# The magic number taken off by TensorE and VectorE instead of Pool in an fp8 rounding stage

## The chip, the cores and the metric
One core of a Trainium2 chip runs the whole kernel. The metric is the device time of one execution in microseconds. The kernel before has a median of 2198.23 us over three runs (2194.11 to 2199.01).

## What is computed
The reference is two transformer layers on x (4 batches x 512 tokens x 512). Only the first of four parts bears on the change:

```python
def _fp8_quant_dequant(x):
    scale = FP8_E4M3_MAX / jnp.maximum(jnp.max(jnp.abs(x)), EPS)
    q = jnp.clip(x * scale, -FP8_E4M3_MAX, FP8_E4M3_MAX).astype(jnp.float8_e4m3fn)
    return q.astype(jnp.float32) / scale
# input = layernorm(x), weight = ctx, bias = mask
out = jnp.einsum('bmk,bkn->bmn', x_dq, w_dq) + bias
x = x + out
```

After it follow a mixture of experts, an attention and a gated feed-forward with a Hadamard transform. They run in later stages of the kernel and are not touched.

## The kernel before
The code writes out, engine by engine, the order of its instructions; there is no planner. Each engine works off its own list and waits on semaphores. The first stage is `batch_product_phase` (L216 to L441); the next stage, `experts_phase`, starts when all engines have left it.

The batches are B = 4 groups of TB = 4 tiles of 128 tokens. SyncE loads x, ctx, the identity and the bias row (broadcast to 128 partitions). VectorE reads the row statistics; the layer norm of three batches is done by ScalarE and of the last by VectorE. VectorE takes the absolute maxima, Pool reduces them over the partitions (L291), and VectorE forms the two scales.

Then eight groups n = 0..7 are quantised, x of batch b being n = 2b and ctx of batch b being n = 2b + 1, each 128 x 2048. The rounding to fp8's three mantissa bits is done by adding and subtracting a large number. ScalarE scales the group (`scale_group`). VectorE's `lift(n)` masks out the exponent of each value (L387), raises it to at least the smallest normal number and multiplies by ROUND_MAGIC (L388), and adds the result to the value (L389). Pool subtracts the same number again and writes bf16 (L303), and VectorE's `clip(n)` bounds the result (L393). TensorE turns the x group with 16 bf16 transposes (L430), ScalarE copies the four turned tiles to SBUF (L337), and TensorE multiplies them with the quantised ctx in 16 matmuls of 512 columns (L438). VectorE's `add(b)` scales the product and adds it to x (L401), and then reads the row statistics of that batch (L102) for the next stage.

Pool adds the bias to x in place (L285): batches 3 and 0 before the all-reduce of the maxima, batch 1 before its first subtraction, batch 2 before its fifth.

In VectorE's list `lift(n)` stands ahead of `clip(n - 1)`, and `add(b - 2)` follows the lift of x of batch b. `scaled`, `magic` and `lifted` have two buffers each, `cq` two, `xq` and `xqT` one.

Two other uses of TensorE with fp32 operands stand in the rows below: `pe.transpose` of fp32 data (L980) and the only plain fp32 `pe.matmul` of the kernel, the router of the experts (L990): 16 tiles times 4 parts, 64 calls, each with 16 moving columns. The products of L52 work on fp32r operands, which a helper splits into a high and a low part.

Of the kernel before, what the change touches and what calls it, by code (L numbers as in the profile page):

```python
# [7 lines left out]
BF16 = mybir.dt.bfloat16  # L8
U32 = mybir.dt.uint32
I32 = mybir.dt.int32  # L10
ALU = mybir.AluOpType
# [3 lines left out]
P = 128  # L15
B, S, D = 4, 512, 512
KD = D // P
# [198 lines left out]
def batch_product_phase(nc, x, ctx_in, bias, consts, x_res, ident, stats):  # L216

    with ExitStack() as ctx:
# [4 lines left out]
        magic = al.sb("magic", [2, TB, D])  # L223
        lifted = al.sb("lifted", [2, TB, D])
        neg_mean = al.sb("neg_mean", [NT])
        xq = al.sb("xq", [TB, D], BF16)
        cq = al.sb("cq", [2, TB, D], BF16)
        xqT = al.sb("xqT", [KD, S], BF16)
        bias_bc = al.sb("bias_bc", [B, D])
        ident_bf = al.sb("ident_bf", [P], BF16)  # L230
# [16 lines left out]
        centred = al.sem("centred")  # L247
        xn_ready = al.sem("xn_ready")
        xn_last = al.sem("xn_last")
        biased = al.sem("biased")  # L250
# [5 lines left out]
        lowered = al.sem("lowered")  # L256
        quant_ready = al.sem("quant_ready")
# [6 lines left out]
        BIAS_ORDER = [B - 1, *range(B - 1)]  # L264
        quantised = lambda n: cq[:, n // 2 % 2] if n % 2 else xq[:, :, :]

        @block.sync
        def _(sp):
# [8 lines left out]
        @block.gpsimd  # L277
        def _(pool):
            pool.wait_ge(bias_in, 16 * B)

            def add_bias(b):
# [6 lines left out]
            for b in BIAS_ORDER[:2]:  # L288
                add_bias(b)
            pool.wait_ge(amax_ready, 1)  # L290
            nc.gpsimd.partition_all_reduce(amax_all[:, :], amax[:, :], P,  # L291
                                           bass.bass_isa.ReduceOp.max).then_inc(amax_over, 1)

            for n in range(2 * B):
                b = n // 2
                if n in (0, 4):
                    add_bias(BIAS_ORDER[2 if n == 0 else 3])
                pool.wait_ge(lifted_ready, n + 1)
                if n % 2 == 0 and b > 0:
                    pool.wait_ge(turned, TB * b)  # L300
                if n % 2 == 1 and b > 1:
                    pool.wait_ge(product, TB * (b - 1))
                pool.tensor_tensor(quantised(n), lifted[:, n % 2], magic[:, n % 2], ALU.subtract).then_inc(lowered, 1)  # L303

        @block.scalar
        def _(act):
            act.wait_ge(neg_mean_ready, 1)
            for g in range(B - 1):
                batch = range(TB * g, TB * g + TB)
                for i in batch:  # L310
                    ins = act.activation(xn[:, i, :], x_res[:, i, :], ACT.Identity, bias=neg_mean[:, i:i + 1])
                ins.then_inc(centred, 1)
                act.wait_ge(centred, g + 1)
# [12 lines left out]

            scale_group(0, xn[:, 0:TB, :], 0)
            scale_group(1, raw[:, 0:TB, :], 1)
            for b in range(B):
                if b + 1 < B:  # L330
                    scale_group(2 * b + 2, xn[:, TB * b + TB:TB * b + 2 * TB, :], 0)
                    scale_group(2 * b + 3, raw[:, TB * b + TB:TB * b + 2 * TB, :], 1)
                if b > 0:
                    act.wait_ge(product, TB * b)
                for t in range(TB):
                    act.wait_ge(turned, TB * b + t + 1)
                    act.activation(xqT[:, :, t * P:(t + 1) * P], turn[t].rearrange("p (k t) -> p k t", k=KD),  # L337
                                   ACT.Copy).then_inc(turned_out, 1)

        @block.vector  # L340
        def _(dve):
# [7 lines left out]
            def batch_amax(which, values, g):  # L349
                return dve.tensor_reduce(amax_parts[:, which, g:g + 1], values[:, TB * g:TB * g + TB, :], AX.XY,  # L350
                                         ALU.max, apply_absolute_value=True)

            for g in range(B):
                dve.wait_ge(x_in[g], 16)
# [21 lines left out]
            dve.wait_ge(scale_ready, 1)  # L376
            link(dve.tensor_tensor(unscale[:, 0:1], scale[:, 0:1], scale[:, 1:2], ALU.mult))
            link(dve.reciprocal(unscale[:, 1:2], unscale[:, 0:1]))

            def lift(n):
                y, m = scaled[:, n % 2], magic[:, n % 2]
# [7 lines left out]
            def clip(n):  # L391
                dve.wait_ge(lowered, n + 1)
                dve.tensor_scalar(quantised(n), quantised(n), FP8_MAX, -FP8_MAX, ALU.min,  # L393
                                  ALU.max).then_inc(quant_ready, 1)

            def add(b):
                dve.wait_ge(biased, BIAS_ORDER.index(b) + 1)
# [6 lines left out]
            lift(0)  # L404
            for n in range(1, 2 * B):
                lift(n)
                clip(n - 1)
                if n >= 4 and n % 2 == 0:
                    add(n // 2 - 2)
                    dve.wait_ge(added, TB * (n // 2 - 1))  # L410
                    stats.read(dve, n // 2 - 2)
            add(B - 2)
            dve.wait_ge(added, TB * (B - 1))
            stats.read(dve, B - 2)
            clip(2 * B - 1)
            stats.finish(dve, 0, B - 1)
            add(B - 1)
            dve.wait_ge(added, NT)
# [3 lines left out]
        def _(pe):  # L422
            pe.wait_ge(const_ready, 1)
            for b in range(B):
                pe.wait_ge(quant_ready, 2 * b + 1)
# [6 lines left out]
                pe.wait_ge(turned_out, TB * (b + 1))  # L432
                pe.wait_ge(quant_ready, 2 * b + 2)
                for t in range(TB):
                    if b > 0:
                        pe.wait_ge(added, TB * (b - 1) + t + 1)
                    for k in range(KD):
                        ins = pe.matmul(banks[t][:, :], xqT[:, k, t * P:(t + 1) * P], cq[:, b % 2, k, :],  # L438
                                        start=(k == 0), stop=(k == KD - 1))
                    ins.then_inc(product, 1)  # L440
    return al.sems  # L441
# [1553 lines left out]
```

## Time and profile before

| | us |
|---|---|
| median of three runs | 2198.23 |
| the profiled execution's own time | 2198.48 |
| its span | 2196.9 |
| TensorE busy | 1963.6 (89%) |
| VectorE busy | 1346.1 (61%) |
| ScalarE busy | 826.8 (38%) |
| Pool busy | 1042.5 (47%) |

The span is the time from the first to the last instruction in the profile; the execution's own time is what the runs' times are compared with. Busy times of a whole kernel are a mean over stages: the first stage takes about the first 145 us, and in it TensorE is mostly idle.

### The profile page before, as it was taken

The page shows a single profiled execution, that of the slowest core. Times are in us where ns is not written, and L with a number is a line of the kernel's source. Part 1 is how long each engine was busy: PE and PEld are TensorE (multiplying, and loading weights), DVE is VectorE, ACT ScalarE, POOL GpSimd, SP SyncE. Part 2 cuts the span into 40 slices and gives each one's busy share as a digit, 9 for nine tenths or more (in the row PEclk, how much of TensorE's full clock was granted, in tenths as well). Part 3 has the DMA queues.
Part 4 walks back from the last instruction along what each step waited for, and adds up shares of the span by engine and source line. Part 5 has one row for each costly group of instructions (what it writes and reads, how often), then busy time and mean ns, then how long its engine had stood idle before and what let it go on. Part 6 is the DMA issues. An engine that isn't in the chain of part 4 may idle for free. (4 is left out here: it accounts for less than half of the span.)

```text
span 2196.9 us, 28789 instructions
## 1 busy us (share of the span) xinstructions
PE 1963.6 (89%) x9721; PEld 1633.4 (74%) x9721; DVE 1346.1 (61%) x2080; ACT 826.8 (38%) x1610; POOL 1042.5 (47%) x837
## 2 busy tenths in 40 slices
PE   0259988784999999999999999999979999999999
PEld 0147766673788888888888888888857788888887
DVE  7885488887677666666776666666666333333333
ACT  4233277772444444444544444444432111111111
POOL 2733635633676666566765666666543222102200
PEclk9869999997999999999999999999999999999999
DMA  4037499984566555556555555555541000000002
GB/s 173 0 118 290 166 320 366 363 312 144 177 184 177 158 148 160 165 148 175 157 162 164 148 160 167 152 149 166 140 121 48 29 29 29 10 19 29 0 1 77
DMA packets 163357, 313.11 MB, mean 143 GB/s; under 512 B 15680, under 2 KB 41024, under 8 KB 163264
## 3 DMA queue, kind: packets, MB, share of 16 engines
q1 hardware_dynamic: 145856, 253.18, 37.6%
q0 software_dynamic: 17408, 58.73, 8.2%
q8 instruction: 53, 0.87, 0.2%
q14 instruction: 40, 0.33, 0.0%
HBM read 203.33 MB, written 108.53 MB: 142 GB/s over the span
## 5 line engine op out<-in xcount | busy, mean ns | idle before, releaser
L1289 POOL TENSOR_TENSOR t_pT_lo<-t_pT_raw,t_pT_hi 128x512 fp32r<-128x512 f32 x256 | 327.3, 1300 | 245.2 <-ACT t_pT_hi L1380 243.4
L1475 DVE TENSOR_REDUCE t_sums<-t_score 128x1 f32<-128x512 f32 x256 | 169.8, 688 | 146.6 <-PE t_score L52 146.5
L1835 DVE TENSOR_TENSOR f_lin<-f_lin,f_silu 128x512 f32<-128x512 f32 x64 | 44.7, 699 | 287.0 <-PE f_lin L52 287.0
L1393 ACT ACTIVATE t_probs<-t_score,t_sums 128x512 f32<-128x512 f32 x256 | 175.0, 683 | 82.7 <-DVE t_sums L1475 67.5
L1465 DVE STREAM_TRANSPOSE t_blocks<-t_probs 128x512 f32<-128x512 f32 x256 | 172.7, 694 | 23.4 <-ACT t_probs L1393 23.1
L1760 POOL TENSOR_TENSOR f_w_hi<-w_raw,f_zeros 128x1024 fp32r<-128x1024 f32 x16 | 30.4, 1903 | 318.3 <-PE f_gate L52 314.8
L1457 DVE SCALAR_TENSOR_TENSOR x_res<-t_out,t_sums,x_res 128x512 f32<-128x512 f32 x256 | 179.2, 741 | 3.7 <-PE t_out L52 3.7
L1380 ACT ACTIVATE t_pT_hi<-t_pT_raw 128x512 fp32r<-128x512 f32 x256 | 160.3, 626 | 5.1 <-DMA t_pT_raw<-turned_blocks 5.1
L1793 ACT ACTIVATE f_silu<-f_gate 128x512 f32<-128x512 f32 x64 | 38.3, 598 | 303.9 <-PE f_gate L52 303.9
L52 PE MATMUL t_score<-t_wv_hi,t_cT_hi 128*128 128x256 f32 x512 | 144.9, 283 | 2.0 <-ACT t_probs L1393 2.0
L52 PE MATMUL t_score<-t_wv_hi,t_cT_lo 128*128 128x256 f32 x512 | 145.0, 283 | 0.0
L52 PE MATMUL t_score<-t_wv_lo,t_cT_hi 128*128 128x256 f32 x512 | 145.0, 283 | 0.0
L1374 ACT ACTIVATE t_o_hi<-t_o 128x512 fp32r<-128x512 f32 x64 | 38.3, 598 | 224.7 <-PE t_o L52 224.7
L1440 DVE TENSOR_TENSOR t_k_lo<-t_score,t_k_hi 128x512 fp32r<-128x512 f32 x64 | 44.3, 692 | 123.5 <-ACT t_k_hi L1365 123.5
L1365 ACT ACTIVATE t_k_hi<-t_score 128x512 fp32r<-128x512 f32 x64 | 38.3, 598 | 212.7 <-PE t_score L52 212.7
L1855 DVE TENSOR_TENSOR x_res<-f_down,x_res 128x512 f32<-128x512 f32 x128 | 87.9, 689 | 42.9 <-PE f_down L52 42.9
L52 PE MATMUL t_score<-t_cT_hi,t_wk_hi 128*128 128x512 f32 x256 | 101.3, 396 | 11.4 <-DVE t_cT_lo L1536 11.4
L52 PE MATMUL t_out<-t_wo_hi,t_o_hi 128*128 128x512 f32 x256 | 103.3, 403 | 8.0 <-DVE t_o_lo L1450 6.3
L52 PE MATMUL t_score<-t_k_hi,t_q_hi 128*128 128x512 f32 x256 | 102.2, 399 | 7.8 <-DVE t_q_lo L1435 4.1
L52 PE MATMUL f_gate<-f_xT_hi,f_w_hi 128*128 128x512 f32 x256 | 101.2, 395 | 8.6 <-POOL f_w_lo L1763 5.5
L52 PE MATMUL t_o<-t_pT_hi,t_v_hi 128*128 128x512 f32 x256 | 100.1, 391 | 4.0 <-POOL t_pT_lo L1289 4.0
L52 PE MATMUL t_q<-t_xT_hi,t_wq_hi 128*128 128x512 f32 x256 | 101.0, 394 | 2.8 <-DVE t_xT_lo L212 2.8
(280 smaller groups left out, 6057.0 us busy)
## 6 DMA issues: line engine op xcount, KB each, us to landing
turned_blocks<-t_blocks SPq DMA_DIRECT2D x256, 256.0 KB, 3.6
t_pT_raw<-turned_blocks SPq DMA_DIRECT2D x256, 256.0 KB, 4.2
e_up_raw<-in_L_ffn_Wrt_up_dram SPq DMA_DIRECT2D x47, 512.0 KB, 7.1
e_down_raw<-in_L_ffn_Wrt_down_dram SPq DMA_DIRECT2D x47, 512.0 KB, 6.3
tokens_by_expert<-e_xg SPq DMA_DIRECT2D x1, 12032.0 KB, 41.1
e_xg<-tokens_by_expert SPq DMA_DIRECT2D x47, 256.0 KB, 6.7
outputs_by_expert<-e_y_out SPq DMA_DIRECT2D x47, 256.0 KB, 7.0
wq_raw<-in_L_xattn_Wq_dram POOLq DMA_DIRECT2D x32, 256.0 KB, 4.3
```

The source lines that it names most:

```text
L52: ins = pe.matmul(out, w(k), x(k), start=(k == 0 and j == 0), stop=(k == k_tiles - 1 and j == 2))
L1289: pool.tensor_tensor(pT_lo[:, q], pT_raw[:, q], f32(pT_hi[:, q]), ALU.subtract).then_inc(p_ready, 1)
L1365: act.activation(k_hi[:, :], score_bank[0][:, :], ACT.Copy).then_inc(k_hi_ready, 1)
L1374: act.activation(o_hi[:, :].rearrange("p (u q j) -> p q u j", q=Q4, j=BLK), o_bank[:, :].rearrange("p (q u j) -> p q u j", q=Q4, j=BLK), A ...
L1380: act.activation(pT_hi[:, q], pT_raw[:, q], ACT.Copy).then_inc(p_hi_ready, 1)
L1393: act.activation(probs[:, t % 2, :], score_bank[t][:, :], ACT.Exp, bias=neg_max[:, t:t + 1], accum_out=inv[:, p, t:t + 1]).then_inc(exp_re ...
L1440: dve.tensor_tensor(k_lo[:, :], score_bank[0][:, :], f32(k_hi[:, :]), ALU.subtract).then_inc(k_ready, 1)
L1457: dve.scalar_tensor_tensor(out=x_tile, in0=out_bank[t % 2][:, :], scalar=inv[:, p, t:t + 1], in1=x_tile, op0=ALU.mult, op1=ALU.add).then_i ...
L1465: dve.transpose(blocks[:, :, :, t, :].rearrange("p a t j -> p t a j"), probs[:, t % 2, :].rearrange("p (t a j) -> p t a j", a=Q4, j=BLK)). ...
L1475: dve.tensor_reduce(neg_max[:, t:t + 1], score_bank[t][:, :], AX.X, ALU.max, negate=True).then_inc(max_ready, 1)
L1835: dve.tensor_tensor(lin_bank[k][:, :], lin_bank[k][:, :], silu[:, k, :], ALU.mult).then_inc(mid_done, 1)
L1855: dve.tensor_tensor(x_tile, down_bank[t][:, :], x_tile, ALU.add).then_inc(added, 1)
```

## The change
Pool's subtraction is gone. `lift` keeps three instructions, but the multiplication by ROUND_MAGIC moves from the second to the third, so that the buffer (now `power`) holds the bare power of two. For x, TensorE turns the lifted value with the identity and adds to the same PSUM tile the turned power times an identity scaled by -ROUND_MAGIC, both as plain fp32 matmuls; the four turn banks are fp32. ScalarE copies them to bf16 as before, and VectorE clips the turned x in one instruction (`clip_x`). For ctx, VectorE takes the magic off itself (`lower_c`) and clips. Two of the four bias additions move from Pool to VectorE. `xqT` has two buffers. VectorE's order per batch is now lift x, lift ctx, lower ctx, clip x, add of the batch before, statistics.

```diff
-        xqT = al.sb("xqT", [KD, S], BF16)
+        xqT = al.sb("xqT", [2, KD, S], BF16)
...
-        turn = [al.ps(f"turn{t}", [KD * P], BF16) for t in range(TB)]
+        turn = [al.ps(f"turn{t}", [KD * P]) for t in range(TB)]
...
+        POOL_BIAS, VECTOR_BIAS = (B - 1, 0), (1, 2)
...
-            for n in range(2 * B):
-                b = n // 2
-                if n in (0, 4):
-                    add_bias(BIAS_ORDER[2 if n == 0 else 3])
-                pool.wait_ge(lifted_ready, n + 1)
-                if n % 2 == 0 and b > 0:
-                    pool.wait_ge(turned, TB * b)
-                if n % 2 == 1 and b > 1:
-                    pool.wait_ge(product, TB * (b - 1))
-                pool.tensor_tensor(quantised(n), lifted[:, n % 2], magic[:, n % 2], ALU.subtract).then_inc(lowered, 1)
...
-            act.activation(ident_bf[:, :], ident[:, :], ACT.Copy).then_inc(const_ready, 1)
+            act.activation(lower_ident[:, :], ident[:, :], ACT.Copy, scale=-ROUND_MAGIC).then_inc(const_ready, 1)
...
             dve.tensor_reduce(amax[:, :], amax_parts[:, :, :], AX.X, ALU.max).then_inc(amax_ready, 1)
+            add_bias(VECTOR_BIAS[0])
             dve.wait_ge(amax_over, 1)
...
             link(dve.reciprocal(unscale[:, 1:2], unscale[:, 0:1]))
+            add_bias(VECTOR_BIAS[1])
+            dve.wait_ge(biased_here, 2)
...
                 dve.wait_ge(scaled_ready, n + 1)
-                if n >= 2:
-                    dve.wait_ge(lowered, n - 1)
+                if n >= 2 and n % 2 == 0:
+                    dve.wait_ge(turned, TB * (n // 2))
                 link(dve.tensor_scalar(m.bitcast(U32), y.bitcast(U32), EXPONENT_BITS, None, ALU.bitwise_and))
-                link(dve.tensor_scalar(m, m, FP8_MIN_NORMAL, ROUND_MAGIC, ALU.max, ALU.mult))
-                dve.tensor_tensor(lifted[:, n % 2], y, m, ALU.add).then_inc(lifted_ready, 1)
...
+                link(dve.tensor_scalar(m, m, FP8_MIN_NORMAL, None, ALU.max))
+                dve.scalar_tensor_tensor(out=lifted[:, n % 2], in0=m, scalar=ROUND_MAGIC, in1=y, op0=ALU.mult,
+                                         op1=ALU.add).then_inc(lifted_ready, 1)
+
+            def lower_c(b):
+                q = cq[:, b % 2]
+                dve.wait_ge(lifted_ready, 2 * b + 2)
+                if b > 1:
+                    dve.wait_ge(product, TB * (b - 1))
+                link(dve.scalar_tensor_tensor(out=q, in0=power[:, 1], scalar=-ROUND_MAGIC, in1=lifted[:, 1], op0=ALU.mult,
+                                              op1=ALU.add))
+                dve.tensor_scalar(q, q, FP8_MAX, -FP8_MAX, ALU.min, ALU.max).then_inc(c_ready, 1)
+
+            def clip_x(b):
+                q = xqT[:, b % 2]
+                dve.wait_ge(turned_out, TB * (b + 1))
+                dve.tensor_scalar(q, q, FP8_MAX, -FP8_MAX, ALU.min, ALU.max).then_inc(x_ready, 1)
...
+            for b in range(B):
+                lift(2 * b)
+                lift(2 * b + 1)
+                lower_c(b)
+                clip_x(b)
+                if b > 0:
+                    add(b - 1)
+                    dve.wait_ge(added, TB * b)
+                    stats.read(dve, b - 1)
...
-                        ins = pe.transpose(turn[t][:, k * P:(k + 1) * P], xq[:, t, k * P:(k + 1) * P], ident_bf[:, :])
+                        ks = slice(k * P, (k + 1) * P)
+                        pe.matmul(turn[t][:, ks], lifted[:, 0, t, ks], ident[:, :], start=True, stop=False)
+                        ins = pe.matmul(turn[t][:, ks], power[:, 0, t, ks], lower_ident[:, :], start=False, stop=True)
```

## Rows read from the trace of the kernel before

**Rows 1.** Windows: stretch, us; busy (x) of PE, PEld, DVE, ACT, POOL; clock; DMA.
```profile
47.50:144.80 97.30, 28.38 (x128) 13.02 (x128) 90.06 (x91) 21.89 (x23) 56.70 (x16) 0.78 0.00 0
```

**Rows 2.** Timeline at the stage's end: start, duration, engine, line, operation, [idle before].
```profile
145.31 4.54 DVE L880 TENSOR_SCALAR e_xn<-x_res,mean_var,rstd 128x512 f32<-128x512 f32 x8 [0.55 <-PEq L218]
```

**Rows 3.** Groups by form, VectorE, 0 to 165 us: busy us, mean ns, idle before.
```profile
L387 DVE TENSOR_SCALAR a_magic<-a_scaled 128x2048 uint32<-128x2048 uint32 x8 | 24.1, 3014 | 1.8 <-ACT a_scaled L324 1.7
L389 DVE TENSOR_TENSOR a_lifted<-a_scaled,a_magic 128x2048 f32<-128x2048 f32 x8 | 20.2, 2527 | 0.3
L388 DVE TENSOR_SCALAR a_magic<-a_magic 128x2048 f32<-128x2048 f32 x8 | 11.7, 1462 | 0.3
L393 DVE TENSOR_SCALAR a_xq<-a_xq 128x2048 bf16<-128x2048 bf16 x4 | 7.0, 1758 | 5.6 <-POOL a_xq L303 5.6
L393 DVE TENSOR_SCALAR a_cq<-a_cq 128x2048 bf16<-128x2048 bf16 x4 | 3.8, 954 | 0.0
```

**Rows 4.** The timeline of VectorE and Pool from 70.5 us.
```profile
70.56 1.22 DVE L387 TENSOR_SCALAR a_magic<-a_scaled 128x2048 uint32<-128x2048 uint32 x1
...
71.81 1.23 DVE L388 TENSOR_SCALAR a_magic<-a_magic 128x2048 f32<-128x2048 f32 x1
73.08 2.29 DVE L389 TENSOR_TENSOR a_lifted<-a_scaled,a_magic 128x2048 f32<-128x2048 f32 x1
75.28 0.69 DVE L393 TENSOR_SCALAR a_cq<-a_cq 128x2048 bf16<-128x2048 bf16 x1
...
75.45 4.90 POOL L303 TENSOR_TENSOR a_xq<-a_lifted,a_magic 128x2048 bf16<-128x2048 f32 x1 [5.36 <-DVE a_lifted L389]
75.89 5.55 DVE L387 TENSOR_SCALAR a_magic<-a_scaled 128x2048 uint32<-128x2048 uint32 x1
...
98.15 2.72 DVE L401 SCALAR_TENSOR_TENSOR x_res<-a_out,a_unscale,x_res 128x512 f32<-128x512 f32 x4
```

**Rows 5.** The timeline around the scales, and one page row for a 128x512 addition's size.
```profile
44.85 0.17 DVE L373 TENSOR_SCALAR a_amax<-a_amax_all 128x2 f32<-128x2 f32 x1 [3.23 <-POOL a_amax_all L291]
47.56 1.23 DVE L387 TENSOR_SCALAR a_magic<-a_scaled 128x2048 uint32<-128x2048 uint32 x1 [1.75 <-ACT a_scaled L324]
...
L1835 DVE TENSOR_TENSOR f_lin<-f_lin,f_silu 128x512 f32<-128x512 f32 x64 | 44.7, 699 | 287.0 <-PE f_lin L52 287.0
```

**Rows 6.** The timeline of ScalarE in the batch of 85 us.
```profile
85.06 2.00 ACT L324 ACTIVATE a_scaled<-a_ctx_raw,a_scale 128x2048 f32<-128x2048 f32 x1 [7.65 <-DVE a_lifted L389]
86.97 2.04 ACT L337 ACTIVATE a_xqT<-a_turn 128x512 bf16<-128x512 bf16 x4
```

**Rows 7.** Groups by form, whole kernel and 145 to 160 us: fp32 matmuls, weight loads.
```profile
L990 PE MATMUL e_bank<-e_router_raw,e_x 128*128 128x16 f32 x128 | 17.9, 289 | 0.0
L980 PE MATMUL e_bank<-ident,e_xn 128*128 128x128 f32 x64 | 11.3, 354 | 4.4 <-DVE e_xn L880 4.4
...
L990 PEld LDWEIGHTS e_bank<-e_router_raw,e_x 128*128 128x128 f32 x60 | 6.9, 192 | 0.0
```

**Rows 8.** The timeline of fp32 bursts; tile queries (starts); windows with granted clock.
```profile
151.79 3.64 PE L990 MATMUL e_bank<-e_router_raw,e_x 128*128 128x16 f32 x32
155.29 1.94 PE L980 MATMUL e_bank<-ident,e_xn 128*128 128x128 f32 x16
...
L990 PE MATMUL e_bank<-e_router_raw,e_x x20: 263/374/376, 167.6 to 171.5; 128*128 128x16 f32 x20
...
L980 PE MATMUL e_bank<-ident,e_xn x22: 401/421/472, 145.9 to 150.5; 128*128 128x128 f32 x22
...
167.80:171.70 3.90, 3.90 (x20) 0.50 1.05 410
```

**Rows 9.** The timeline of split products and of this stage's last turn.
```profile
704.46 0.28 PE L52 MATMUL t_score<-t_wv_hi,t_cT_hi 128*128 128x256 f32 x1
...
705.17 0.28 PE L52 MATMUL t_score<-t_wv_hi,t_cT_hi 128*128 128x256 f32 x1
...
129.41 1.17 PE L430 MATMUL a_turn<-a_ident_bf,a_xq 128*128 128x128 bf16 x16 [4.35 <-DVE a_xq L393]
```

More of the change, by code:

```diff
@@ L222, in batch_product_phase @@
         scaled = al.sb("scaled", [2, TB, D])
[L223 removed]
+        power = al.sb("power", [2, TB, D])
         lifted = al.sb("lifted", [2, TB, D])
         neg_mean = al.sb("neg_mean", [NT])
[L226 removed]
         cq = al.sb("cq", [2, TB, D], BF16)
[L228 removed]
+        xqT = al.sb("xqT", [2, KD, S], BF16)
         bias_bc = al.sb("bias_bc", [B, D])
[L230 removed]
+        lower_ident = al.sb("lower_ident", [P])
         amax_parts = al.sb("amax_parts", [2, B])
@@ L249, in batch_product_phase @@
         xn_last = al.sem("xn_last")
-        biased = al.sem("biased")
+        biased, biased_here = al.sem("biased"), al.sem("biased_here")
         amax_ready = al.sem("amax_ready")
@@ L255, in batch_product_phase @@
         lifted_ready = al.sem("lifted_ready")
-        lowered = al.sem("lowered")
-        quant_ready = al.sem("quant_ready")
+        c_ready = al.sem("c_ready")
+        x_ready = al.sem("x_ready")
         turned = al.sem("turned")
@@ L263, in batch_product_phase @@
         tiles = lambda a, g: a[g].rearrange("(t p) d -> p t d", p=P)
-        BIAS_ORDER = [B - 1, *range(B - 1)]
-        quantised = lambda n: cq[:, n // 2 % 2] if n % 2 else xq[:, :, :]
+        POOL_BIAS, VECTOR_BIAS = (B - 1, 0), (1, 2)
         @block.sync
@@ L279, in _ @@
             pool.wait_ge(bias_in, 16 * B)
-            def add_bias(b):
+            for b in POOL_BIAS:
                 pool.wait_ge(*((xn_ready, b + 1) if b + 1 < B else (xn_last, 1)))
@@ L286, in add_bias @@
                 ins.then_inc(biased, 1)
-            for b in BIAS_ORDER[:2]:
-                add_bias(b)
             pool.wait_ge(amax_ready, 1)
@@ L332, in _ @@
                     scale_group(2 * b + 3, raw[:, TB * b + TB:TB * b + 2 * TB, :], 1)
-                if b > 0:
-                    act.wait_ge(product, TB * b)
+                if b > 1:
+                    act.wait_ge(product, TB * (b - 1))
                 for t in range(TB):
                     act.wait_ge(turned, TB * b + t + 1)
-                    act.activation(xqT[:, :, t * P:(t + 1) * P], turn[t].rearrange("p (k t) -> p k t", k=KD),
+                    act.activation(xqT[:, b % 2, :, t * P:(t + 1) * P], turn[t].rearrange("p (k t) -> p k t", k=KD),
                                    ACT.Copy).then_inc(turned_out, 1)
@@ L351, in batch_amax, with add_bias @@
                                          ALU.max, apply_absolute_value=True)
+            def add_bias(b):
+                dve.wait_ge(bias_in, 16 * B)
+                for t in range(TB):
+                    x_tile = x_res[:, TB * b + t, :]
+                    ins = dve.tensor_tensor(x_tile, x_tile, bias_bc[:, b, :], ALU.add)
+                ins.then_inc(biased_here, 1)
             for g in range(B):
@@ L378, in _ @@
             link(dve.reciprocal(unscale[:, 1:2], unscale[:, 0:1]))
+            add_bias(VECTOR_BIAS[1])
+            dve.wait_ge(biased_here, 2)
             def lift(n):
-                y, m = scaled[:, n % 2], magic[:, n % 2]
+                y, m = scaled[:, n % 2], power[:, n % 2]
                 dve.wait_ge(scaled_ready, n + 1)
-                if n >= 2:
-                    dve.wait_ge(lowered, n - 1)
+                if n >= 2 and n % 2 == 0:
+                    dve.wait_ge(turned, TB * (n // 2))
                 link(dve.tensor_scalar(m.bitcast(U32), y.bitcast(U32), EXPONENT_BITS, None, ALU.bitwise_and))
-                link(dve.tensor_scalar(m, m, FP8_MIN_NORMAL, ROUND_MAGIC, ALU.max, ALU.mult))
-                dve.tensor_tensor(lifted[:, n % 2], y, m, ALU.add).then_inc(lifted_ready, 1)
[L391 to L394, printed above, removed]
+                link(dve.tensor_scalar(m, m, FP8_MIN_NORMAL, None, ALU.max))
[4 more added lines that the diff above has]
+                dve.wait_ge(lifted_ready, 2 * b + 2)
+                if b > 1:
+                    dve.wait_ge(product, TB * (b - 1))
[6 more added lines that the diff above has]
+                dve.tensor_scalar(q, q, FP8_MAX, -FP8_MAX, ALU.min, ALU.max).then_inc(x_ready, 1)
             def add(b):
-                dve.wait_ge(biased, BIAS_ORDER.index(b) + 1)
+                dve.wait_ge(biased, len(POOL_BIAS))
                 for t in range(TB):
@@ L402, in add @@
                                              in1=x_res[:, i, :], op0=ALU.mult, op1=ALU.add).then_inc(added, 1)
[L404 to L415, printed above, removed]
+            for b in range(B):
[7 more added lines that the diff above has]
+                    stats.read(dve, b - 1)
             stats.finish(dve, 0, B - 1)
@@ L424, in _ @@
             for b in range(B):
-                pe.wait_ge(quant_ready, 2 * b + 1)
+                pe.wait_ge(lifted_ready, 2 * b + 1)
                 for t in range(TB):
@@ L429, in _ @@
                     for k in range(KD):
-                        ins = pe.transpose(turn[t][:, k * P:(k + 1) * P], xq[:, t, k * P:(k + 1) * P], ident_bf[:, :])
+                        ks = slice(k * P, (k + 1) * P)
+                        pe.matmul(turn[t][:, ks], lifted[:, 0, t, ks], ident[:, :], start=True, stop=False)
+                        ins = pe.matmul(turn[t][:, ks], power[:, 0, t, ks], lower_ident[:, :], start=False, stop=True)
                     ins.then_inc(turned, 1)
-                pe.wait_ge(turned_out, TB * (b + 1))
-                pe.wait_ge(quant_ready, 2 * b + 2)
+                pe.wait_ge(c_ready, b + 1)
+                pe.wait_ge(x_ready, b + 1)
                 for t in range(TB):
@@ L437, in _ @@
                     for k in range(KD):
-                        ins = pe.matmul(banks[t][:, :], xqT[:, k, t * P:(t + 1) * P], cq[:, b % 2, k, :],
+                        ins = pe.matmul(banks[t][:, :], xqT[:, b % 2, k, t * P:(t + 1) * P], cq[:, b % 2, k, :],
                                         start=(k == 0), stop=(k == KD - 1))
```

## The prediction

> **What bounds the kernel now.** I read the page's busy shares first, then the windows of the first stage, the groups of instructions by form in that stage, its timeline, and last TensorE's rows for fp32 operands wherever the kernel has them. The change lies wholly in the first stage, and the chain that ended last names no line of it, so what binds here has to be read from the stage itself. From the first rounding instruction to the last row statistics VectorE works 90.06 of 97.30 us while TensorE has 28.38 and ScalarE 21.89 [rows 1]. VectorE's last statistics end at 144.76 (145.31 less 0.55 of idle), and what releases its first instruction of stage two is the branch at the barrier [rows 2]. What the first stage ends earlier or later should therefore move the whole rest, one for one.
>
> VectorE's 90 us are not all its own work. The same masking instruction L387 takes 1.22 us at 70.56, when Pool is idle, and 5.55 us at 75.89, when a Pool subtraction of 4.90 us has just begun; it ends 1.1 us after Pool does, as if it had waited for Pool's end [rows 4]. So I take a clean time for each form from [rows 4] and compare it with the group sums of [rows 3].
>
> **Term A, what goes.** The groups L387, L388, L389 and the two of L393 take 24.1 + 11.7 + 20.2 + 7.0 + 3.8 = 66.8 us [rows 3]. Without Pool beside them: 8 x (1.22 + 1.23 + 2.29) + 8 x 0.69 = 43.4 [rows 4]. Both lifts stay three instructions of the same size, and both clips stay (the x clip moves behind the turn, same 128x2048 bf16 shape), so the gain is 23.4. VectorE's wait for Pool's subtraction goes too, 5.6 [rows 3]. A = -29.0. The subtraction on Pool itself (eight like the 4.90 at 75.45) is gone with nobody waiting for it.
>
> **Term B, what VectorE gets.** lower_c is a fused multiply-add of 128x2048 fp32 into bf16, four times. The fused form appears at 128x512 as 2.72 for four, PSUM operand included, and the plain fp32 tensor_tensor at 128x2048 takes 2.29 [rows 4]. Bounds 2.29 and 2.72; I take 2.29, the same element count without PSUM. With its link: 4 x 2.33 = +9.3. The last multiplication of the lift moves from the second instruction into the third; both sizes and counts of passes are as before, so 0.
>
> **Term C, the bias.** Two of Pool's four bias batches go to VectorE, 4 x 0.70 = 2.8 us each, by the 128x512 fp32 tensor_tensor [rows 5]. The first stands where VectorE idles 3.23 before the all-reduce's answer at 44.85 [rows 5]: hidden. If Pool's all-reduce is slowed by it, at most doubled, that is +3. The second stands where VectorE now waits 1.75 for ScalarE's scaled x [rows 5]: 2.8 - 1.75 = +1.05, and the wait for its own writes makes it +1.1. No DMA moves: SyncE's queue issues what it did, and the bias rows have landed well before 44.85, since Pool, which waits for them first of all, answers then.
>
> **Term D, the new wait.** clip_x(b) sits in VectorE's queue and waits for turned_out, that is for TensorE's turn in fp32 and ScalarE's copies. Behind it are queued add, the row statistics, the next lift, and TensorE's product. Count from L, the end of lift(2b). VectorE reaches clip_x at L + 4.72 (lift(2b+1), 70.56 to 75.28) + 2.33 + 0.65 = L + 7.7. ScalarE scales the next context group from L + 4.8 to L + 6.8 and then needs 2.04 for four copies [rows 6]: L + 8.9 at best, a floor of 1.2 us of waiting in the first three batches.
>
> TensorE is the unknown. The code issues 32 plain fp32 matmuls a batch. L990 is the only plain fp32 matmul in the trace: 64 in the code, 128 records, so each is two records with a weight load each, where the 64 fp32 transposes of L980 are 64 records [rows 7]. So 64 records a batch. Their pitch: L990, with only 16 moving columns, (3.64 - 0.26) / 31 = 0.109 us in a warm stretch, and about 0.21 at the half clock (20 records from 167.6 to 171.5, granted 0.50, 1.2 of 2.4 GHz) [rows 8]. That hardly depends on the columns, since the transposes with 128 columns have the same two pitches, (1.94 - 0.27) / 15 = 0.111, and 22 records from 145.9 to 150.5, 0.22: the weight load sets L990's pitch. A load's record there lasts 192 ns, reaching over the next load's start [rows 7]. In the split products of 256 columns, one load each, the pitch is (705.17 - 704.46) / 6 = 0.118 [rows 9]: there 256 columns stream under one load. If a record of the new turn streams its 128 columns twice, it is that same case: 0.118. Bounds: below 0.109, above load and stream not overlapped, 0.109 + 0.109 = 0.218.
>
> The clock: between product and turn TensorE will rest some 4 to 6 us. After a rest of 4.4 before 145.91 L980 starts at a pitch of 0.22 and keeps it 4.6 us [rows 7, 8]. I take 4.5 us, 21 records, at 1.2 GHz and 43 at 2.4: 4.5 + 43 x 0.118 + 0.27 = 9.85. The copy of the last tile is out at L + 0.1 + 9.85 + 0.6 + 0.1 = L + 10.65, so clip_x waits 2.95. Four batches: D = +11.8. Product and add keep their places and hide as before: product(3) runs beside add(2), the statistics and the finish, 9 us for its 6.
>
> The Trainium skill has a rule that speaks against the change: "TensorE: Matmul & The Clock Gate", section "Terms", says transpose mode makes fp32 four times faster, and the change gives that mode up. Taken at its word a plain one would cost 4 x 0.109 = 0.436, two records of 0.218, rival 2 below. "FP8 and Floating Point Precision", section "TensorE Precision Notes", counts four passes for true fp32, two a record, which would fit under the load and give the sum above. No row here decides between them.
>
> **Sum.** -29.0 + 9.3 + 1.1 + 11.8 = -6.8. The profiled execution took 2198.48 around a span of 2196.9, 0.25 above the median of the three runs, 2198.23. 2198.48 - 6.8 = 2191.7.
>
> **Rivals.**
> 1. The turn is cheaper: TensorE stays at 2.4 GHz and the pitch is 0.109. 64 x 0.109 + 0.27 = 7.25, the copies end at ScalarE's floor, waits 1.2 x 3 and 0.35 in the last: 3.95 for 11.8, so 2183.8. For it: the turn at 129.41 ran 16 bf16 records in 1.17, warm after a rest of 4.3 [rows 9]. Against: the rest before 145.91.
> 2. The slower side: load and stream don't overlap, 0.218 a record, 0.43 at the low clock. 4.5 + 53.5 x 0.218 + 0.27 = 16.4, wait 9.5 a batch, 38.0 for 11.8: +19.4, 2218. VectorE then waits on TensorE. It decides from where the waits sum over 18.6, 4.65 a batch, a turn of 11.55 us. For it: no row shows 128 plain columns. Against: L990's pitch equals one load, so loads do run under streams.
> 3. Pitch as forecast, but the clock never rises in the turn: 64 x 0.213 = 13.6 + 0.27, wait 7.0, sum 28: +9.4, 2208. Against: L980 rises within its burst.
> 4. No change: the clock rises 8 us into the turn, or the pitch is some 0.145: wait 4.5, sum 18, 2198. Also where Pool isn't what stretches L387, half of A gone and the turn short.
>
> **How the numbers follow.** Forecast 0.59, its own range 2188 to 2195 (clock 3 to 6.5 us low, waits 2.3 to 3.8, 2 us of scatter); rival 1 0.10; rival 2 0.11; rival 3 0.07; rival 4 0.13. 0.2% is 4.4 us, what can be told from no change here. Faster: nearly all of the first two cases less the forecast's edge, 0.66. Within: rival 4 and that edge, 0.16. Slower: rivals 2 and 3, 0.18. The range 2183.5 to 2204 leaves out rival 2, most of rival 3 and the low end of rival 1.
>
> **What would show it.** In the stage's groups after: L387's counterpart at 1.22 mean and no instruction over 3 us; lower_c at 2.3; 256 records of the turn at 0.12 pitch once the clock is granted; VectorE idle before clip_x about 3 us four times, released by ScalarE's copy; second stage starting near 138.5. A turn of over 11.5 us a batch, or masks still over 2 us with Pool silent, would make it wrong.

## The result, and the profile after

The kernel after takes 2184.02 us, the median of four runs (2180.46 to 2187.84); the kernel before, four runs on the same chip, 2197.65 (2194.11 to 2199.01). The ratio is 0.9941 with a 95% interval of 0.992 to 0.9961: about 13 us faster, more than the 4.4 us that this kernel's measurement can tell from nothing. The forecast was 2191.7. The profiled executions took 2180.46 after and 2198.48 before. Of all executions behind the ratios below one is left out as disturbed, of bias_only: 3075.57 us, where its eleven others took 2218 to 2230.

The windows of the first stage after, from its first mask to its last statistics, answer to [rows 1]; columns as there.

```profile
48.39:132.68 84.29, 47.58 (x316) 39.23 (x320) 76.23 (x95) 21.43 (x23) 0.00 (x0) 0.91 0.00 0
```

VectorE's busy time falls from 90.06 to 76.23, Pool's from 56.70 to nothing, and TensorE's rises from 28.38 to 47.58. VectorE is still the engine that sets the length, but in 8 us of the 84 it now stands idle.

The groups by form on VectorE from 44 to 165 us after, answering to [rows 3]: busy us, mean ns, then idle before.

```profile
L382 DVE SCALAR_TENSOR_TENSOR a_lifted<-a_power,a_scaled 128x2048 f32<-128x2048 f32 x8 | 18.3, 2293 | 0.3
L381 DVE TENSOR_SCALAR a_power<-a_power 128x2048 f32<-128x2048 f32 x8 | 9.8, 1227 | 0.3
L380 DVE TENSOR_SCALAR a_power<-a_scaled 128x2048 uint32<-128x2048 uint32 x8 | 9.8, 1222 | 0.1
L390 DVE SCALAR_TENSOR_TENSOR a_cq<-a_power,a_lifted 128x2048 bf16<-128x2048 f32 x4 | 9.2, 2292 | 0.1
L397 DVE TENSOR_SCALAR a_xqT<-a_xqT 128x2048 bf16<-128x2048 bf16 x4 | 2.8, 694 | 6.5 <-ACT a_xqT L321 6.5
L392 DVE TENSOR_SCALAR a_cq<-a_cq 128x2048 bf16<-128x2048 bf16 x4 | 2.8, 694 | 0.1
```

The mask has gone from a mean of 3014 ns to 1222, and every form now has one duration. The one new idle time is the 6.5 us ahead of the clip of the turned x, L397, released by ScalarE's copy.

The timeline after, at the places of [rows 5], [rows 6] and [rows 2] and at the four waits.

```profile
44.86 0.17 DVE L365 TENSOR_SCALAR a_amax<-a_amax_all 128x2 f32<-128x2 f32 x1 [1.14 <-POOL a_amax_all L286]
45.85 2.50 DVE L341 TENSOR_TENSOR x_res<-x_res,a_bias_bc 128x512 f32<-128x512 f32 x4
48.39 1.23 DVE L380 TENSOR_SCALAR a_power<-a_scaled 128x2048 uint32<-128x2048 uint32 x1
62.92 0.69 DVE L397 TENSOR_SCALAR a_xqT<-a_xqT 128x2048 bf16<-128x2048 bf16 x1 [1.94 <-ACT a_xqT L321]
75.01 2.04 ACT L321 ACTIVATE a_xqT<-a_turn 128x512 bf16<-128x512 f32 x4
77.08 0.69 DVE L397 TENSOR_SCALAR a_xqT<-a_xqT 128x2048 bf16<-128x2048 bf16 x1 [0.96 <-ACT a_xqT L321]
97.24 0.69 DVE L397 TENSOR_SCALAR a_xqT<-a_xqT 128x2048 bf16<-128x2048 bf16 x1 [1.70 <-ACT a_xqT L321]
117.56 0.69 DVE L397 TENSOR_SCALAR a_xqT<-a_xqT 128x2048 bf16<-128x2048 bf16 x1 [1.85 <-ACT a_xqT L321]
133.23 4.54 DVE L882 TENSOR_SCALAR e_xn<-x_res,mean_var,rstd 128x512 f32<-128x512 f32 x8 [0.55 <-PEq L218]
```

The stage ends at 133.23 - 0.55 = 132.68, 12.1 us earlier than the 144.76 of before. The profiled spans differ by 18.1 (2196.9 and 2178.8). The other 6 lie in later stages: from the experts to the attention 239.2 us before and 236.2 after, from there to the feed-forward 1145.4 and 1142.3. Over all kernels profiled here these two stretches range over 236.2 to 241.1 and 1141.6 to 1145.4, with nothing in them changed. Two more profiles of the changed kernel (after_again and after_third below) have 239.7 and 1144.9, 238.6 and 1145.3, so the shorter stretches of this one are scatter. What the change did by the profiles is the 12.1; the 13.6 between the medians agrees with it within the interval.

The windows of PE in the four turns after: stretch and length, busy (records), granted clock, DMA share, GB/s. (A turn is TensorE's 64 records for one batch.) The first row is nearly the whole of the second turn, the other two pairs are the third and the fourth, each cut where its clock rose.

```profile
68.70:75.50 6.80, 6.80 (x63) 1.00 0.01 2
...
87.85:90.50 2.65, 2.65 (x12) 0.50 0.00 0
90.60:96.30 5.70, 5.70 (x53) 0.99 0.01 3
...
108.00:111.10 3.10, 3.10 (x14) 0.50 0.00 0
111.20:116.60 5.40, 5.40 (x50) 1.00 0.00 0
```

All of it is 64 records a batch, about 0.11 us apart at 2.4 GHz and 0.21 to 0.22 at 1.2. The four turns last 8.91, 7.42, 8.77 and 8.90 us, with some 3.1, 0.3, 2.7 and 3.15 of them at the lower pace. For the third and fourth the granted clock of the rows says so. For the first two it doesn't, the view has 1.00 throughout: the first turn's 3.1 us are read from its records, which start 0.213 apart until 56.5 and 0.112 after, and in the second only the first record is followed after 0.21, which costs 0.1 us.

### The profile page after: what moved, and what is told of

It reads as the page before. It is cut to its first block and busy times, and to the rows that moved or that the text cites. A ratio compares the mean times of both kernels' runs of the same rounds, so it can differ in the third digit from the quotient of the medians.

```text
span 2178.8 us, 29158 instructions
## 1 busy us (share of the span) xinstructions
PE 1979.0 (91%) x9909; PEld 1655.4 (76%) x9913; DVE 1338.5 (61%) x2092; ACT 826.4 (38%) x1610; POOL 991.1 (45%) x821
```

## The experiments

A kernel's ratio is to the kernel before on the same chip, with its 95% interval. Times of different chips are not compared: where half_turn, double_turn, warm and pool_beside ran, the kernel before takes 2198, elsewhere some 2226, with the expert stage about 28 us longer in every kernel. Stage one is compared by the start of stage two, the first `e_xn` row of the timeline, which is 133.23 in the change.

**The change again, twice.**

> The changed kernel once more, beside the other three on one chip. The first stage ended at 144.76 us before and at 132.68 after, 12.1 earlier; the profiled spans differ by 18.1. Theory (all of the gain is made in the first stage): the ratio to before is 1 - 12.1/2198 = 0.9945, 2186 us, and the 6 us more of the profiled pair are scatter of the expert stage. Rival (something behind the first stage gains too): ratio near 0.992, 2180 us.

> The changed kernel once more, as the measure for the two beside it: stage one over at 132.7 to 134.3, the second stage's wait for the router 28.94 us after its start, ratio to before 0.993 to 0.9945.

after_again: 0.9926 (0.9903 to 0.9949), stage two starts at 134.80, waits 2.72, 0.96, 1.98 and 2.13. after_third: 0.9954 (0.9936 to 0.9972), 133.17, waits 1.91, 0.96, 1.68 and 1.85. Both intervals hold the 0.9945 of the stage alone; that of after_again holds the rival's 0.992 too, that of after_third doesn't. Between copies of one kernel the start of stage two moves by 1.6 us, 1.4 of it through the three waits that hang on the turn (the first turn of after_again took 9.69 us); the 0.96 stays.

**Is it Pool's silence? Pool kept busy with work that nobody waits for.**

```diff
+            for n in range(2 * B):
+                pool.wait_ge(lifted_ready, n + 1)
+                pool.wait_ge(idle_done, n) if n else None
+                pool.tensor_tensor(idle_out[:, :, :], bias_bc[:, :, :], bias_bc[:, :, :], ALU.subtract).then_inc(idle_done, 1)
```

> The changed kernel, and beside it Pool does a 128x2048 fp32 subtraction into an unused bf16 tile each time a lift is done, as it did before the change; nobody waits for it. Theory (Pool's mere running stretches VectorE): the mask after each lift of x goes from 1.2 to 5.5 and the ctx clip is held to Pool's end, some 4.3 + 2.6 a batch, 27.6 us, less the waits that it covers, 6.45: stage end near 154, ratio to before 1.004. Rival (the stretch came from what both touched, or the gain came from shorter dependencies): VectorE's instructions stay at 1.22 and 2.29, ratio 0.9945.

1.0062 (1.0048 to 1.0077), slower than before; stage two starts at 152.54, 19.3 us later than in the profile of after. The profiled execution took 2201.83, the other three 2210.39 to 2213.16; what the further 9 to 11 us are, no profile shows. The timeline of VectorE and Pool in it:

```profile
97.61 1.22 DVE L386 TENSOR_SCALAR a_power<-a_scaled 128x2048 uint32<-128x2048 uint32 x1
97.77 4.51 POOL L293 TENSOR_TENSOR a_idle_out<-a_bias_bc 128x2048 bf16<-128x2048 f32 x1 [11.22 <-DVE a_lifted L388]
98.86 4.50 DVE L387 TENSOR_SCALAR a_power<-a_power 128x2048 f32<-128x2048 f32 x1
...
105.73 2.29 DVE L396 SCALAR_TENSOR_TENSOR a_cq<-a_power,a_lifted 128x2048 bf16<-128x2048 f32 x1
105.77 5.70 POOL L293 TENSOR_TENSOR a_idle_out<-a_bias_bc 128x2048 bf16<-128x2048 f32 x1 [3.49 <-DVE a_lifted L388]
108.05 3.97 DVE L398 TENSOR_SCALAR a_cq<-a_cq 128x2048 bf16<-128x2048 bf16 x1
```

The mask that began before Pool's instruction keeps its 1.22. The tensor_scalar that begins after it takes 4.50 for 1.23 and ends at 103.36, 1.08 after Pool's 102.28: it waits for Pool's end. The fused instruction with two inputs runs beside Pool in its usual 2.29, and there it is Pool that pays, 5.70 for 4.51. The clip that follows it, L398, begins during Pool's instruction and is held again, 3.97 for 0.69. The buffers are unrelated, so no dependence of data does this. The Trainium skill says this under "SBUF — State Buffer", section "Who interferes with whom": GpSimd and a tensor_scalar of VectorE in its faster mode exclude each other for a whole instruction, and whichever has begun first keeps the port. The trace agrees, with 4.50 for 1.23.

**One part alone: the bias of batches 1 and 2 to VectorE in the kernel before.**

```diff
...
             dve.tensor_reduce(amax[:, :], amax_parts[:, :, :], AX.X, ALU.max).then_inc(amax_ready, 1)
+            add_bias(VECTOR_BIAS[0])
...
+            add_bias(VECTOR_BIAS[1])
+            dve.wait_ge(biased_here, 2)
```

In Pool's list, which stands earlier in the file:

```diff
-                if n in (0, 4):
-                    add_bias(BIAS_ORDER[2 if n == 0 else 3])
```

> The kernel before with one part of the change alone: the bias of batches 1 and 2 is added by VectorE at the same places as in the changed kernel; Pool still subtracts the magic. Theory: VectorE's wait of 5.6 us for Pool's first subtraction goes, and the stretches beside Pool's two long bias additions; the masks beside Pool's subtractions stay at 5.5. Counted through, the stage ends near 138.2, 6.6 earlier, ratio 0.997. Rival (Pool's subtraction is the whole cost): no gain beyond 1 us, ratio 1.0.

0.9963 (0.9946 to 0.9981); stage two starts at 138.57, 6.7 us before [rows 2]. So about half of the gain needs neither TensorE's part nor Pool's leaving the subtraction, only two bias additions moved. VectorE no longer waits for Pool's subtraction, because Pool is never behind, but it is stretched nearly as before: its rounding groups sum to 64.9 us where [rows 3] have 66.8. The group of its mask in bias_only, and one meeting with Pool in its timeline:

```profile
L395 DVE TENSOR_SCALAR a_magic<-a_scaled 128x2048 uint32<-128x2048 uint32 x8 | 27.1, 3384 | 0.1
```

```profile
53.70 5.40 POOL L301 TENSOR_TENSOR a_xq<-a_lifted,a_magic 128x2048 bf16<-128x2048 f32 x1 [8.47 <-DVE a_lifted L397]
54.78 5.41 DVE L396 TENSOR_SCALAR a_magic<-a_magic 128x2048 f32<-128x2048 f32 x1
```

Here L396 ends 1.09 after Pool does, once more.

**The other way to free Pool: VectorE lowers x as it lowers the context, and TensorE turns bf16.**

```diff
+            def lower_x(b):
+                q = xq[:, :, :]
...
+                link(dve.scalar_tensor_tensor(out=q, in0=power[:, 0], scalar=-ROUND_MAGIC, in1=lifted[:, 0], op0=ALU.mult,
+                                              op1=ALU.add))
                 dve.tensor_scalar(q, q, FP8_MAX, -FP8_MAX, ALU.min, ALU.max).then_inc(x_ready, 1)
...
-                        pe.matmul(turn[t][:, ks], lifted[:, 0, t, ks], ident[:, :], start=True, stop=False)
-                        ins = pe.matmul(turn[t][:, ks], power[:, 0, t, ks], lower_ident[:, :], start=False, stop=True)
+                        ins = pe.transpose(turn[t][:, k * P:(k + 1) * P], xq[:, t, k * P:(k + 1) * P], ident_bf[:, :])
```

> The changed kernel with TensorE's part undone: VectorE takes the magic off x as well (a fourth fused instruction per batch, 2.29 us, and a clip of bf16 before the turn), TensorE turns bf16 as before; Pool stays out. Theory (the gain comes from Pool's leaving, TensorE's subtraction only saves 4 x 2.33 us of VectorE less the 6.45 us of waits): stage end 48.4 + 61.6 + 15.8 + 9.3 = 135.0, +2.3 against the changed kernel, ratio to before 0.9955. Rival (TensorE's part carries the gain): the stage ends near 144 again, ratio 1.0.

0.9962 (0.9944 to 0.9981); stage two starts at 136.19, 1.4 us after after_again and 3.0 after after_third. The group of the added instruction:

```profile
L398 DVE SCALAR_TENSOR_TENSOR a_xq<-a_power,a_lifted 128x2048 bf16<-128x2048 f32 x4 | 9.2, 2292 | 0.1
```

That is 9.2 us of VectorE's own work in place of 6.45 to 7.8 of waits for the turn: TensorE's share in the change is worth 1.4 to 3 us. The rest, 9.1 us from [rows 2], comes with Pool out of the loop, whether the magic is then taken off by TensorE or by VectorE; bias_only has 6.7 of them with Pool still subtracting. The intervals of the ratios overlap with those of the change, so it is read from the starts alone.

**What does the turn cost VectorE? The turn halved and doubled.** half_turn leaves out the second matmul of each pair (so the large number stays on x), double_turn issues each pair twice.

```diff
-                        pe.matmul(turn[t][:, ks], lifted[:, 0, t, ks], ident[:, :], start=True, stop=False)
-                        ins = pe.matmul(turn[t][:, ks], power[:, 0, t, ks], lower_ident[:, :], start=False, stop=True)
+                        ins = pe.matmul(turn[t][:, ks], lifted[:, 0, t, ks], ident[:, :], start=True, stop=True)
```

> The changed kernel without the second matmul of each pair (the magic stays on x: that part of the computation is left out). The turn halves to 64 records less 32: about 5.4 us cold, 3.8 warm. Theory (VectorE's wait at the clip is the longer of TensorE's turn and ScalarE's copies, and ScalarE alone leaves a floor of about 1 us in batches 0 to 2): waits 1.2 + 1 + 1 + 0 for 6.45, stage end near 129.4, 3.3 earlier, ratio to before 0.993. Rival (there is no floor, TensorE alone sets the wait): waits 0, 126.2.

> The changed kernel with every pair of turning matmuls issued twice (same result), 128 records a batch. Theory (above 6.95 us every us of the turn is a us of waiting): turn 3.3 + 112 x 0.1115 + 0.3 = 16.1 cold-started and 14.5 warm, waits 9.1 or 7.5, 33 to 37 us in sum for 6.45, stage end near 161, 28 later, ratio to before about 1.007. Rival (the wait is soaked up elsewhere, by the add and the statistics behind it): under 15 us later.

half_turn: 0.9923 (0.9909 to 0.9938), start of stage two 129.74. double_turn: 1.0083 (1.0063 to 1.0103), 162.77. The clips' rows, first of half_turn, then of double_turn:

```profile
62.11 0.69 DVE L397 TENSOR_SCALAR a_xqT<-a_xqT 128x2048 bf16<-128x2048 bf16 x1 [0.96 <-ACT a_xqT L321]
...
114.07 0.69 DVE L397 TENSOR_SCALAR a_xqT<-a_xqT 128x2048 bf16<-128x2048 bf16 x1
```

```profile
71.01 0.69 DVE L397 TENSOR_SCALAR a_xqT<-a_xqT 128x2048 bf16<-128x2048 bf16 x1 [10.05 <-ACT a_xqT L321]
91.70 0.69 DVE L397 TENSOR_SCALAR a_xqT<-a_xqT 128x2048 bf16<-128x2048 bf16 x1 [7.50 <-ACT a_xqT L321]
```

With the turn out of the way 0.96 is left three times and nothing the fourth: that is ScalarE, which scales the next context before it copies, and has none to scale in the last batch. Stage two starts 3.5 us earlier than in after, for 6.45 - 2.88 = 3.6 less of waiting. (In this profile stage two then loses more than that again, see late_clip below.) Twice the turn brings 29.5 us, for 36.00 - 6.45 = 29.55 more of waiting. So the waits go into the length of the stage one for one, and the turn counts only above ScalarE's floor.

**What does a record cost, by its columns?** Plain fp32 matmuls of eight widths, twelve of each, ahead of the first turn, behind twenty of 128 columns.

```diff
...
+            for n in (16, 64, 96, 128):
+                for f in range(12):
+                    pe.matmul(turn[f % TB][:, 0:n], ident[:, :], ident[:, 0:n], start=True, stop=True)
+            for n in (192, 256, 384, 512):
+                for f in range(12):
+                    pe.matmul(turn[f % TB][:, 0:n], ident[:, :], bias_bc[:, 0, 0:n], start=True, stop=True)
```

> The changed kernel with bursts of 12 plain fp32 matmuls (24 records) of 16, 64, 96, 128, 192, 256, 384 and 512 moving columns on TensorE ahead of the first turn, behind 20 of 128 columns that raise the clock; only the pitch of records within a burst is read, the kernel's own time means nothing. Theory (a record is the longer of a weight load of 0.107 us and two streams of its columns at 2.4 GHz): 0.11 up to 128 columns, 0.160 at 192, 0.213 at 256, 0.320 at 384, 0.427 at 512. Rival (load and stream add up, at one column a cycle in sum 0.107 for 128): pitch falls below 0.09 at 64 and 16 columns and grows evenly, 0.16 at 256, 0.27 at 512. Rival (four streams a record): 0.213 already at 128.

Only its rows are read. TensorE's records by tile in narrow stretches: line, count, shortest/median/longest in ns, first and last start, forms.

```profile
L429 PE MATMUL a_turn<-ident x26: 274/276/352, 54.6 to 57.5; 128*128 128x128 f32 x24, 128*128 128x96 f32 x2
L432 PE MATMUL a_turn<-a_bias_bc,ident x24: 326/327/328, 57.7 to 61.4; 128*128 128x192 f32 x24
L432 PE MATMUL a_turn<-a_bias_bc,ident x24: 326/380/380, 61.4 to 66.3; 128*128 128x256 f32 x23, 128*128 128x192 f32 x1
L432 PE MATMUL a_turn<-a_bias_bc,ident x25: 379/487/487, 66.5 to 74.2; 128*128 128x384 f32 x24, 128*128 128x256 f32 x1
L432 PE MATMUL a_turn<-a_bias_bc,ident x25: 486/593/593, 74.2 to 84.3; 128*128 128x512 f32 x24, 128*128 128x384 f32 x1
```

Each matmul is two records. Their pitch at 2.4 GHz is 0.112 us at 128 columns, 0.1625 at 192, 0.216 at 256, 0.3225 at 384 and 0.429 at 512. From 192 on that is two cycles of 2.4 GHz a column: 2 x 192 / 2400 = 0.160, 2 x 512 / 2400 = 0.427. At 128 columns it would be 0.107, but the bursts of 16 and 64 columns stood at 0.112 as well, and the router's 16 at 0.109 [rows 8]. So a record takes two cycles a column and never less than about 0.11. That this floor is the load of the next weights, which lies beside the stream, fits these numbers; no run varies the load alone. "FP8 and Floating Point Precision" of the Trainium skill, section "TensorE Precision Notes", counts four passes for true fp32; two records of two cycles a column are four, and this trace agrees. The Trainium skill's rule in "TensorE: Matmul & The Clock Gate", section "Terms", that transpose mode is four times faster in fp32, does not hold at 128 columns: two records of 0.1115 are 0.223, twice the 0.111 of a transpose [rows 8].

The windows of PE in columns. The first runs from the middle of the burst of 64 columns to near the end of that of 96, the second over that of 128; before 47.9 the bursts of 16 and 64 columns ran at a granted 1.00.

```profile
48.00:54.60 6.60, 6.60 (x33) 0.50 0.00 0
55.00:57.60 2.60, 2.60 (x26) 1.00 0.00 0
```

**Can the clock be held up? Filler matmuls ahead of each turn.**

```diff
+                if b > 0:
+                    pe.wait_ge(turned_out, TB * b)
+                for f in range(50 if b == 0 else 16):
+                    pe.matmul(turn[f % TB][:, 0:P], ident[:, :], ident[:, :], start=True, stop=True)
```

> The changed kernel with filler matmuls on TensorE (50 plain fp32 ones before the first turn, 16 before each other, into the same banks, overwritten). Theory (the turns of batches 0, 2 and 3 lose 1.3 to 1.6 us each to the low clock): turns all 7.4 us, waits at ScalarE's floor 1.1 x 3 + 0.5, 3.6 for 6.45, stage end near 130, ratio to before 0.993. Rival (fillers delay the turns, or the clock doesn't rise for them): no gain or a loss against 0.9945.

0.9957 (0.9938 to 0.9975); stage two starts at 132.53, waits 1.98, 2.64, 0.96 and 0.35, in sum 5.93 for 6.45, and no gain in time over the change. The theory mostly failed. In the first batch the fillers ended at 50.57, TensorE rested 2.50, and then the clock fell inside the turn, from 54.5 to 57.7; before the second turn, which needs no help, the fillers delayed it. The last two turns did fall to their floors.

**Can the wait be filled? The clip moved behind the add and the statistics of the batch before.**

```diff
-                clip_x(b)
                 if b > 0:
                     add(b - 1)
                     dve.wait_ge(added, TB * b)
                     stats.read(dve, b - 1)
+                clip_x(b)
```

> VectorE's clip of the turned x stands behind the add and the statistics of the batch before, instead of ahead of them; nothing else. Theory (VectorE's waits at the clip, 0.96 + 1.70 + 1.85 us in batches 1 to 3, are the only cost of the turn, and 5.2 us of other work covers them): the stage ends 4.5 earlier, at 128.2, ratio to before 0.9925; batch 0 keeps its wait of 1.9. TensorE's rest before each turn shrinks from 5.6 to about 1, so the turn starts at 2.4 GHz. Rival (the later clip makes the product late for the add, or delays the next turn): the wait moves to the add, no gain over the changed kernel, 0.9945.

0.9936 (0.991 to 0.9961), against 0.9926 of after_again beside it: no gain. Yet the stage is shorter, with waits of 3.01, 0, 0 and 0. TensorE goes into the last two turns almost without a rest, and they take 7.31 us each, with no record at the low pace. Rows of late_clip:

```profile
129.93 4.50 DVE L882 TENSOR_SCALAR e_xn<-x_res,mean_var,rstd 128x512 f32<-128x512 f32 x8 [0.90 <-PEq L218]
...
130.78 5.29 PE L982 MATMUL e_bank<-ident,e_xn 128*128 128x128 f32 x32 [5.38 <-DVE e_xn L882]
148.59 13.67 PE L992 MATMUL e_bank<-e_router_raw,e_x 128*128 128x16 f32 x64
...
162.30 0.43 DVE L831 TENSOR_REDUCE e_top<-e_bank 128x16 f32<-128x256 f32 x1 [17.49 <-PE e_bank L992]
```

The same in after:

```profile
133.84 5.96 PE L982 MATMUL e_bank<-ident,e_xn 128*128 128x128 f32 x32 [11.16 <-DVE e_xn L882]
...
151.57 10.56 PE L992 MATMUL e_bank<-e_router_raw,e_x 128*128 128x16 f32 x64
...
162.17 0.42 DVE L831 TENSOR_REDUCE e_top<-e_bank 128x16 f32<-128x256 f32 x1 [14.01 <-PE e_bank L992]
```

Stage two starts 4.9 us before after_again's, and `e_top`, which needs the router, comes 32.37 us after that start, not 28.94: the last 64 router records take 13.67 for 10.56, the pitch of the lower clock. In after, before and six of the other profiles it is 28.94 or 28.95, in warm 28.91. But half_turn has 35.24 (its profiled execution took 2187.5, two of its others 2179), and columns has 38.35, though it starts stage two last of all, at 164.41. So an early end of stage one alone doesn't explain the loss.

**Late only in batches 1 and 2, so that TensorE's rest before stage two is as in the change; and the same with a bias addition in batch 0's wait.**

```diff
+                late = b in (1, 2)
+                if not late:
+                    clip_x(b)
...
+                if late:
+                    clip_x(b)
```

> The late clip only in batches 1 and 2; batches 0 and 3 as in the changed kernel. Theory (the late clip of all three batches won 4.9 us in stage one and lost 3.4 again at the router of stage two, because TensorE then rested only 5.4 us ahead of that stage and its clock fell at another place): with batch 3's clip early TensorE's rest before stage two is 11 us again, the router's wait 28.94, and stage one still ends 2.7 to 2.9 earlier: ratio 0.0013 under the changed kernel's. Rival (any earlier end of stage one is given back at the router): router's wait 31 to 32, ratio equal to the changed kernel's.

> As late_mid, and VectorE's bias of batch 2 stands in its wait for the first turn (1.9 to 3.0 us) instead of ahead of the first lift. Theory: the first lift starts at 47.6 instead of 48.4, the wait of batch 0 takes the 2.5 us of the bias: 0.4 to 0.8 us less than late_mid. Rival (the turn starts 0.8 earlier only, and the wait outlasts the bias): within 0.3 of late_mid.

late_mid: 0.9951 (0.9932 to 0.997), late_mid_bias: 0.995 (0.993 to 0.997), beside after_third's 0.9954. Stage two starts at 131.02 and 130.20, waits 2.78, 0, 0, 1.37 and 0.70, 0, 0, 1.47. The bias in the wait brought the 0.8 expected of it. In late_mid the rest was restored, 11.15 us, and the clock was not. The timeline and window of late_mid:

```profile
131.62 6.37 PE L986 MATMUL e_bank<-ident,e_xn 128*128 128x128 f32 x32 [11.15 <-DVE e_xn L886]
155.65 13.67 PE L996 MATMUL e_bank<-e_router_raw,e_x 128*128 128x16 f32 x64
...
169.36 0.42 DVE L835 TENSOR_REDUCE e_top<-e_bank 128x16 f32<-128x256 f32 x1 [23.41 <-PE e_bank L996]
```

```profile
144.00:169.00 25.00, 25.00 (x121) 0.50 1.05 411
```

From 144 on TensorE runs at a granted 0.50, 96 of the router's 128 records in it, and `e_top` comes 38.34 us after the stage's start (38.35 in late_mid_bias). My theory, that the length of TensorE's rest before stage two decides this, fell; after one and the same rest of 9.48 us warm has 28.91, half_turn 35.24 and columns 38.35. The runs of late_mid go from 2207.0 to 2220.8, those of after_third from 2210.1 to 2225.3. Six runs of late_mid took 2217.4 or more and one 2207.0, about the 9.4 us that the profiled one lost at the router; whether that one kept its clock, no profile shows. So none of the three orders is seen to beat the change in time, though they start stage two 2.1 to 3.2 us earlier than its best copy. What sets the router's clock stays open.

## Why the prediction was right, and where it was off

Direction and path were forecast well, the size only to a factor of two: 13.6 us by the medians where 6.5 were forecast, 12.1 in the stage where 6.8 were. The 2184.02 lies inside the stated range by 0.5 us at its lower end, one of the four runs lies below it, and the forecast's own case, 2188 to 2195 with a chance of 0.59, did not come. That the time fell inside is in part luck.

What binds and where it ends: right. Stage one ends earlier and stage two follows it, 28.94 us to `e_top` in both kernels.

Term A, -29.0: right. The groups' 9.8 + 9.8 + 18.3 + 2.8 + 2.8 are 43.5 against the 43.4 worked out from [rows 4], and no wait for Pool is left, so -23.3 and -5.6. pool_beside puts the stretch back with a Pool instruction that nobody needs, and so shows that the stretch is Pool's doing and not that of the order of the lift's instructions. Only the account by instruction was too simple: what is hit is whichever tensor_scalar begins during Pool's instruction, the mask as well as the one behind it or the clip.

Term B, +9.3: right, 4 x 2.29 = 9.2. The lower bound held because the output in bf16 and the fused form cost nothing over [rows 4]'s 2.29.

Term C, +1.1: right, 0.8. The first bias lies in the wait for the all-reduce, which shrinks from 3.23 to 1.14 while its answer stays at 44.86; the first mask starts at 48.39 for 47.56. 2.50 for the four instructions, not 2.8.

Term D, +11.8: this is the step that was mis-sized. It measured 1.94 + 0.96 + 1.70 + 1.85 = 6.45. The mechanism is as forecast, 64 records, a start at the lower clock (in three of the four turns), the copy as releaser, and the offset too: a turn of 8.91 leaves a wait of 1.94, 6.97 less, where 9.85 was to leave 2.95, 6.90 less. What was too large are two sizes in the turn. The lower clock was taken for 4.5 us in each batch, 18 in all, from the rest before 145.91; it lasted 3.1, 0.3, 2.7 and 3.15, 9.25 in all (12.4 in after_again, whose waits are 7.8). A microsecond there costs 1 - 0.1115 / 0.2133 = 0.48, so that is 4.2 of the miss. And the pitch was taken as the 0.118 of the split products, where it is 0.1115: some 48 records x 4 x 0.0065 = 1.2. Together 5.4, the miss; the four turns took 34.0 us where 39.4 were forecast. In the second batch the turn is so short (7.42) that ScalarE releases the clip, and the floor, put at 1.2, is 0.96.

The sum with the measured terms is -28.9 + 9.2 + 0.8 + 6.45 = -12.4, for 12.1 seen, where -6.8 was forecast. The other 6 us between the profiles, of later stages, were in no term. Of the rivals, the cheaper turn, given 0.10, came nearest: 2183.8, with waits of 3.95 where 6.45 were measured. The low clock was short and not absent, and that the two times agree to 0.2 us is chance. Load and stream one after the other (rival 2), and with it the fourfold price of a plain matmul, fell with the columns: 0.112 at 128 for its 0.218. A clock that never rises (rival 3) was seen in no turn of the change. double_turn shows that the price of the slow side was real: 36.0 us of waits make the kernel slower than before by 0.8%.

## What to carry to other kernels

When Pool and VectorE share a stage, look for a VectorE tensor_scalar whose mean is well above its shortest and that ends a fixed bit after a Pool instruction (1.1 us here for the fp32 ones). Pool's instruction then costs VectorE time even where nobody waits for its result: 19.3 us here. Work moved to an idle TensorE costs only what its chain (turn, copy) exceeds the floor that another engine sets, and the copy's place in that engine's list is part of the floor. In the three profiles of the change the turns that TensorE began after a rest of 4.3 to 5.6 us ran 2.7 to 3.8 us at the lower pace, those after 1.0 us only their first record. In the other runs, after rests of 3.1 to 4.1, it was anything from that to 6.1. So take the rest and the low stretch from the nearest burst, let the range hold both ends, and look at the granted clock of the next stage before booking a saved microsecond.

## What the hardware showed that was not expected

The granted clock fell to 0.50 from 48.0 to 54.6 in columns while TensorE had 6.60 us of 6.60 busy with narrow fp32 matmuls of 64 and 96 columns back to back. The columns alone don't decide it: the bursts of 16 columns and the first records of 64 just before had run at 1.00. It was 0.50 in late_mid too, for the 25 us from 144 to 169, all back-to-back records, most of them the router's of 16 columns, at a DMA share of 1.05. TensorE had no idle time in either stretch. The same 64 records of the router ran in 10.56 us in the change and 13.67 in late_mid.

A plain fp32 matmul of 16 columns costs what one of 128 does: 0.112 us a record each in columns.
